# Attention and feed-forward on one core: TensorE's side work of a unit placed between its two score steps

## What is computed

```python
def _L0_attn_ref(hidden, ...):
    x = hidden
    x = x + global_latent_attn(rmsnorm(x, norm1_w), ...)   # causal over all 1024 keys
    x = x + local_gqa_attn(rmsnorm(x, norm2_w), ...)       # window of 32 keys
    return x
...
x = x + ga * _L0_attn_ref(h, ...)
h = _layernorm(x, axis=-1) * (1 + cb) + sb
x = x + gb * _L0_ffn_ref(h, ...)
```

## Time and profile before

| | us |
|---|---|
| median of 3 runs | 1261.52 (1261.52 to 1261.7) |
| the profiled execution's own time | 1260.0 |
| its span, first to last instruction | 1258.2 |
| TensorE matmuls busy | 1115.9 (89%) |
| VectorE busy | 977.6 (78%) |
| ScalarE busy | 814.8 (65%) |
| GpSimd busy | 427.7 (34%) |
| mean granted TensorE clock | 0.963 |

### The profile page before, as it was taken

How to read it: one execution, slowest core, us unless ns; L and a number is a source line. 1 busy time by engine, 2 the same in 40 slices (tenths; PEclk the granted TensorE clock), 3 DMA queues, 4 the chain that set the end, 5 groups by cost and what they waited for, 6 DMA issues and landing times.

```text
span 1258.2 us, 37452 instructions
## 1 busy us (share of the span) xinstructions
PE 1115.9 (89%) x15987; PEld 695.4 (55%) x16018; DVE 977.6 (78%) x1540; ACT 814.8 (65%) x1197; POOL 427.7 (34%) x568
## 2 busy tenths in 40 slices
PE   4488889898987968678999999999999999999985
PEld 3133434343444746455666666666666666666662
DVE  7869684868778588897887888788778877887755
ACT  3498898989886857346555755575566566656541
POOL 1203221211203527765533433343333333333310
PEclk8599999999999989889999999999999999999997
DMA  3114121022122532101211110110111101111102
GB/s 107 34 22 139 46 95 35 18 101 85 50 85 70 164 117 86 51 18 27 74 28 23 28 27 19 23 36 20 24 26 24 28 22 27 28 23 27 27 7 67
DMA packets 41685, 61.71 MB, mean 49 GB/s; under 512 B 7441, under 2 KB 16817, under 8 KB 41521
## 3 DMA queue, kind: packets, MB, share of 16 engines
q1 hardware_dynamic: 39728, 58.44, 15.9%
q10 hardware_dynamic: 1792, 0.87, 0.3%
HBM read 22.61 MB, written 16.78 MB: 31 GB/s over the span
## 4 chain that ended last, share of the span: by engine, by line
PE 51%; DVE 4%; ACT 2%; issue 1%; DVEq 0%; ACTq 0%
PE psum L1386 9%; PE psum L1522 7%; PE psum L1475 6%; PE psum L1497 5%; PE psum L1461 5%; PE psum L1396 4%; PE psum L1406 4%; PE psum L1548 3%; PE psum L1483 2%; PE psum L1446 2%; PE psum L1418 2%; ACT ffn_probs L1705 2%; PE psum L1452 1%; PE psum L1426 1%; PE psum L1514 1%
## 5 line engine op out<-in xcount | busy, mean ns | idle before, releaser
L876 ACT ACTIVATE att_probs<-psum 128x1024 f32<-128x1024 f32 x352 | 335.1, 1028 | 44.2 <-PE psum L732 43.7
L1816 POOL TENSOR_TENSOR ffn_rot<-ffn_rot,ffn_rot_sin 128x512 f32<-128x512 f32 x128 | 160.1, 1272 | 372.0 <-DVE ffn_rot L1847 371.9
L775 PE MATMUL psum<-att_probs,att_v 128*32 128x256 f32 (+3 forms) x3072 | 178.8, 348 | 3.7 <-DVE att_probs L1068 3.1
L732 PE MATMUL psum<-att_q_stack,att_k_parts 64*128 64x512 bf16 (+2 forms) x1472 | 133.7, 274 | 51.2 <-ACT att_probs L876 32.5
L732 PEld LDWEIGHTS psum<-att_q_stack,att_k_parts 64*128 64x128 bf16 x1472 | 45.7, 95 | 141.6 <-ACT att_probs L876 103.5
L1068 DVE TENSOR_TENSOR att_probs<-att_probs,att_causal_mask 128x1024 f32<-128x1024 f32 (+1 forms) x80 | 95.8, 1213 | 32.2 <-ACT att_probs L876 32.0
L1698 ACT ACTIVATE ffn_max_t<-psum 68x128 bf16<-68x128 bf16 x64 | 17.5, 273 | 156.7 <-PE psum L1434 156.6
L775 PEld LDWEIGHTS psum<-att_probs,att_v 128*32 128x32 f32 x3072 | 79.8, 110 | 62.5 <-issue 37.9
L1705 ACT ACTIVATE ffn_probs<-psum 128x1024 f32<-128x1024 f32 x64 | 65.6, 1025 | 59.2 <-PE psum L1461 59.2
L1667 ACT ACTIVATE ffn_sq<-psum 128x512 f32<-128x512 f32 x128 | 74.5, 595 | 21.1 <-PE psum L1386 20.0
L662 POOL TENSOR_TENSOR att_rot<-att_qk 128x1280 f32<-128x1280 f32 x6 | 16.5, 2755 | 195.1 <-ACT att_qk L907 195.1
(11 more groups left out here) (226 smaller groups left out, 2458.8 us busy)
## 6 DMA issues: line engine op xcount, KB each, us to landing
ffn_v_back<-ffn_v SPq DMA_DIRECT2D x120, 130.0 KB, 2.4
att_q_stack<-q_rows SPq DMA_DIRECT2D x28, 512.0 KB, 3.8
q_rows<-att_q_high SPq DMA_DIRECT2D x21, 256.0 KB, 2.8
q_rows<-att_q_mid SPq DMA_DIRECT2D x21, 256.0 KB, 3.1
q_rows<-att_q_low SPq DMA_DIRECT2D x14, 256.0 KB, 3.8
xres<-in_hidden SPq DMA_DIRECT2D x4, 512.0 KB, 6.0
out<-ffn_qk_t SPq DMA_DIRECT2D x3, 512.0 KB, 3.2
tail_f_wqkv<-in_f_wqkv SPq DMA_DIRECT2D x1, 768.0 KB, 5.7
```

Source lines behind the costliest of these rows:

```text
L732: ins = T.matmul(psum[:, banks[i] + at:banks[i] + at + width], k_parts[rows, p % 3, j, key:key + P], q_stack[rows, turn % 2, j, q0:q0 + wi ...
L775: ins = T.matmul(psum[32 * g:32 * g + V_PAD, (4 + cc) * BANK + lo - cc * BANK: (4 + cc) * BANK + hi - cc * BANK], v_of(p, kt, g, shift), p ...
L876: act.activation(probs[:, n % E_BUFS, 2 * j:2 * j + 2, 0:width], ps2((step % 2) * 2).rearrange("p (h c) -> p h c", h=2)[:, :, 0:width], AC ...
L1816: steps.did(pool.tensor_tensor(out, out, halves(k.rot_sin[:, n % 2, :])[:, :, 1 - half, :], ALU.add), g["added"] if half else None)
```

## The change

In TensorE's loop the side work moves from behind the values to between the two score steps. No operation, wait or table is added or taken away; the loops of the other engines stay as they are.

```diff
             for n in range(FIRST_TICK, LAST_TICK):
-                for j in range(2):
-                    if 0 <= n < n_units:
-                        scores(n, j)
-                for j in range(2):
-                    if 0 <= n - LAG < n_units:
-                        values(n - LAG, j)
+                if 0 <= n < n_units:
+                    scores(n, 0)
                 for j in range(2):
                     for p in qkv_on_pe("transpose", n):
...
                         transposes(side, post_rows[b], share_of(n, n, j, TILES), nt_in_psum)
+                if 0 <= n < n_units:
+                    scores(n, 1)
+                for j in range(2):
+                    if 0 <= n - LAG < n_units:
+                        values(n - LAG, j)
```

## The result

| | before | after |
|---|---|---|
| median, us | 1261.52 (1258.25 to 1261.7) | 1302.08 (1297.96 to 1304.9) |
| the profiled execution's own time | 1260.0 | 1304.8 |
| its span | 1258.2 | 1302.9 |
| mean granted TensorE clock | 0.963 | 0.949 |

The ratio is 1.0325, 95% interval 1.0286 to 1.0364: the change makes the kernel slower by 40.6 us. The forecast was 1285 in a range of 1265 to 1299. The sign was right; the size was not.

What follows compares the result with a forecast made beforehand. Global stretch bound by TensorE and ScalarE handing work to each other, local by waiting along chains. Losses 8.6 (11.5 less 2.9) plus 15.0, 23.6 us on 1260.0, give 1283.6; the median stands 1.5 higher: 1285, range 1265 to 1299.

Steps and rivals of the forecast that it cites:

- The hole: TensorE's short wait for an exponential before the second score step, which side work would fill; 0.28 us in one tick type.
- Part 1: Global units: filling the wait between score steps gains 2.9 us, from twelve lone side ticks after tick 38.
- Ticks 63, 70, 86 to 110 and 161 to 163: Places where waiting side work delays scores, exponentials and copies: losses of 1.7, 1.0, 1.3 and 5.1 us.
- 0 to 2 us, taken as 0: Local stretch: the second scores and values following side work at the low TensorE clock; priced at nothing in the sum.
- larger loss: Rival: delays reach the queries' DMA spread and the low clock covers more stretches; 10 to 15 us more, 1297; chance 0.16.
- Part 3: Local units: no hole to fill, only waits moved, in four blocks of ticks; 15.0 us lost.
- 147 to 156: Local block: scores and values behind waiting side work, then copies behind held exponentials, delay growing tick by tick to 6.0 us.
- 164 to 171: Local block of back-to-back hand-ons of ScalarE and VectorE; 1.0 us lost.
- the end of attention: Ticks 172 to 178: masks and the tail's gated addition 3.4 us later, of which 2.9 arrive at the tail's end.
- Part 2: Global units: waiting side work holds the second scores, exponential and values; 11.5 us lost over the dense places.
- Ticks 118 to 120: Global units: transposes, then two projections handing on through copies behind held exponentials; 2.7 us lost.
- the feed-forward half stays at 738: Sign: the feed-forward half holds no line of the change, so its 738 us stay unchanged.

Runs made afterwards that it cites:

- ssxv: Against the kernel before, every tick runs both score steps, then side work, then values: 1271.43 us, ratio 1.0088.
- lone_only: The kernel before with the new order only in 19 global ticks whose side work had its operands ready: 1257.23 us, ratio 0.9980.
- warm_fitted: The changed kernel with TensorE repeating score matmuls in its waits before side work, local repeats cut to a third: 1294.70 us, ratio 1.0270 to the kernel before.
- global_only: The kernel before with the new order only in ticks below 144, the global units: 1271.63 us, ratio 1.0091.
- local_only: The kernel before with the new order only from tick 144 on, the local units: 1286.01 us, ratio 1.0209.
- before_filled: The kernel before, order unchanged, with TensorE's idle time filled by repeated matmuls at ticks 37, 148, 161 and 177: 1262.82 us, ratio 1.0016.
- block161_old: The changed kernel with ticks 161 and 162 alone back in the old order: 1290.76 us, ratio 1.0241 to the kernel before.

## Why the prediction was right, and where it failed

**Right: the order and what is held.** The hole is filled, but S1, E1 and all that stands behind them wait whenever X waits; ScalarE's wait for scores grows (24.9 to 51.6 us); side work comes to wait for the copies (L1014 and L1030 in the rows above); tick 62's side work starts 2.2 us after its S0; VectorE gets a gap of 4.1 us at tick 161, where about 3 was forecast. ssxv shows the held S1 as the cause of 30 of the 40.6 us, their clock included, and lone_only the gain of the hole, 3.6 us against the 2.9 of Part 1.

**Right in size: the waits at the high clock.** Ticks 63, 70, 86 to 110 and 161 to 163 came out at 1.7, 1.0, 1.3 and 5.0 us where the record has 1.7, 1.0, 1.3 and 5.1, once the clock was kept high (warm_fitted). At 161 to 163 that is partly luck: the record reckoned with transposes of 1.97 us and a stall of 3.6 on VectorE, and warm_fitted has 1.09 and 2.80, and more behind them.

**The step that failed: the clock, "0 to 2 us, taken as 0".** The prediction looked only at stretches that already were low in the trace of before, and priced S1 and V standing in one of them. It did not ask what the new gaps do. Between 65 us and the end of attention, the kernel before has four low stretches, 20 us together; the changed one has twelve, 58 us. The new ones lie behind gaps that the change makes, of 1.7 us (at 112.5 and 328.4), 1.8 (194.6), 2.0 (378.7) and more. Not every such gap is followed by one: after gaps of 1.5 us (212.8 and 442.1) and 1.7 (420.8 and 464.7) the clock stayed high, nor was there one behind gaps of 3.3 and 2.1 us (392.8 and 440.7) in the kernel before. So the theory put on record with global_only, a low stretch behind each new gap over about 1.5 us, does not hold as a rule, and no run here gives one. In the global stretch four of the five cost 0.7 to 1.5 us each, since S1 and the values stand right behind the side work. Kept high, the clock takes 8.6 us off the profiled execution's attention half (40.5 to 31.9) and 6.9 us off the total by the ratios. The profiled execution is one of the changed kernel's two slower ones (1304.8 us at a mean granted clock of 0.949; the other two took 1298.0 and 1299.4 at 0.957 and 0.955), so its 8.6 may be above what the clock costs this kernel on average. The rival "larger loss" named the mechanism but expected it only behind 7 us waits, and as a case of 0.16; it belonged into the sum. On this the Trainium skill (TensorE: Matmul & The Clock Gate, HAM oscillation — how this bites in real kernels) describes the pattern: TensorE throttles to half rate in a wait between bursts, so that each burst starts slow. The rows agree with the pattern, and show it here behind gaps of 1.7 to 2.0 us, though not behind each of them.

**Mis-sized: Part 3.** With 5.0 us at 161 to 163, the other three blocks were short. 147 to 156 was followed tick by tick but left out ScalarE's square at tick 152 (7.2 in local_only where the record has 6.0; the changed kernel's 8.9 has another 1.6 at tick 156, where its low stretch at 449.7 lies); 164 to 171 measured 2.3 for 1.0; and the end of attention 5.0 to 6.1 for 2.9, where I had assumed that the order of the tail hides part of it. Its last rows show how the clock enters there too, first in the changed kernel, then in the one before:

```profile
555.26 3.49 PE L849 MATMUL psum<-tail_space 128*128 128x128 f32 x16 [1.79 <-ACT tail_space L939]
```

```profile
516.71 2.02 PE L853 MATMUL psum<-tail_space 128*128 128x128 f32 x16 [0.24 <-ACT tail_space L938]
```

The last output projection, which took 2.02 us, takes 3.49; VectorE waits for it with its last addition (L1056), and the feed-forward half starts about a microsecond behind that.

**Missed: a place in Part 2.** Tick 132 steps by 1.3 us, in both traces of the table (within its row 130 to 139); the blocks on record have nothing between 119 and 133. From 132 to 139 the trace at the high clock then has 2.8 us, where the record has 3.4. Ticks 118 to 120 measured 3.3 at the high clock for 2.7.

**Wrong: "the feed-forward half stays at 738".** It takes 741.8 us from its first matmul instead of 737.6. Nearly all of it (3.7) is lost in its first 130 us: its 1500th matmul starts 133.1 us after the first instead of 129.4. The clock is low there five times, 11.6, 18.4, 45.7, 59.4 and 73.0 us after the first matmul (20.5 us together), and in the kernel before twice, after 10.3 and 58.1 (17.1 us together). The losses step near the two places that the kernel before has not, by 1.5 us between the 300th and 400th matmul and by 1.7 between the 600th and 700th. Every other version but before_filled (737.7) also takes longer here than the kernel before, 738.7 to 740.2, whether its attention ends earlier or later, and every one of them has a low stretch 69.6 to 73.0 us after its first matmul, also where the first two lie as in the kernel before (lone_only, ssxv). What decides whether it comes is open: no run was made on that.

**In sum**, for the profiled executions, 44.8 us against 23.6 on record: 8.6 is the clock in attention, 4.2 the feed-forward half, and the remaining 8.4 the waits that Parts 2 and 3 had too small or not at all. The last is an upper bound, since warm_fitted's repeats themselves hold work in the local stretch. Each term compares two single executions.

## What to carry to other kernels

When an instruction stream is reordered, ask of the moved work not whether it fills a hole but whether it can wait, and what is queued behind it: here side work that waits for a copy was put ahead of the step that releases the copy's engine. Price a new wait on TensorE once for its length and, as a term with a chance, once more for the matmuls behind it at half the clock. Such an order pays only where the operands are ready: restricted to nineteen ticks the kernel was 3.4 us faster, and everywhere it cost 40.6.

## What the runs showed of the hardware

- A TensorE gap of 1.74 us was followed by a low-clock stretch, and the same place with a gap of 1.04 us was not; eight projection matmuls took 2.72 and 1.57 us. Splitting the gap with two idle score steps, into 0.85 and 0.29 us, restored 1.57.
- The length of the gap did not decide it alone. Gaps of 1.72 and 1.98 us before the same projections were followed by a low stretch in the profiled execution of the changed kernel and not in that of block161_old.
- A low-clock stretch on TensorE's path cost 0.7 to 1.5 us in five cases in the global units (four in the changed kernel, one in lone_only). One whose work VectorE was behind with anyway cost nothing in the end (tick 163 of before_filled).
- The changed kernel's own executions lie at 1298 and 1299 us with a mean granted clock of 0.957 and 0.955, and at 1305 twice with 0.949. The time goes with the clock there; that the clock alone makes the 6 us is not shown. Executions of the kernel before at 0.963 and 0.964 lie from 1257.8 to 1263.3 us.
